# A value product moved into three norm stretches, relational maxima taken one by one, and a bank of their own for the first places

## The reference, cut to what matters

```python
# block 0, node layers (3 of them) and kernel attention; both start from the same xn
for l in range(L):
    msgs = nodes[src] + nodes[dst] + edge_proj
    agg = jax.ops.segment_sum(msgs, dst, num_segments=n)
    h = jnp.concatenate([nodes, agg], axis=-1) @ W1[l].T + b1[l]
    h = jax.nn.relu(_layernorm(h, ln_g[l], ln_b[l]))
    nodes = h @ W2[l].T + b2[l] + nodes
...
qkv = x @ qkv_w.T + qkv_b                       # x = xn: does not depend on the node layers
phi_q = jnp.exp(jnp.einsum('bhnd,md->bhnm', q, rf) - q_norm)
phi_k = jnp.exp(jnp.einsum('bhnd,md->bhnm', k, rf) - k_norm)
kv = jnp.einsum('bhnm,bhnd->bhmd', phi_k, v)
# block 1, relational attention, twice (4 heads, 1 head), 3 relations
alpha = jax.nn.leaky_relu(qi + kj, NEG_SLOPE)
m = jax.ops.segment_max(alpha, dst, num_segments=n_nodes)
e = jnp.exp(alpha - m[dst])
# block 3, experts: 16 experts each take their 64 best nodes
topk_score, topk_ids = jax.lax.top_k(scores.T, capacity)
xg = x[topk_ids]
```

## Time and profile before

| | |
|---|---|
| median of 3 runs | 4625.5 us |
| the profiled execution's own time | 4628.15 us |
| its span, first to last instruction | 4626.4 us |
| TensorE matmul busy | 4411.0 us (95%) |
| VectorE, ScalarE busy | 1027.6 us (22%), 1007.6 us (22%) |
| mean granted TensorE clock | 0.982 |
| data moved | 795.72 MB, mean 172 GB/s |

### The profile page before, as it was taken

One profiled execution on the slowest core, in us unless ns is written; L12 is line 12 of the kernel. 1 busy time (PEld: TensorE's weight loads), 2 busy tenths in 40 slices (PEclk: granted clock), 3 DMA queues, 4 the chain that ended last, 5 costly groups with the idle time before them and its releaser, 6 DMA issues.

```text
span 4626.4 us, 37973 instructions
## 1 busy us (share of the span) xinstructions
PE 4411.0 (95%) x15158; PEld 1976.2 (43%) x15183; DVE 1027.6 (22%) x1909; ACT 1007.6 (22%) x1830; POOL 89.9 (2%) x169
## 2 busy tenths in 40 slices
PE   8999999999999997989999999999999999999998
PEld 3444444444445543444444444443444334333333
DVE  6872011212311226123300000022542000000000
ACT  3121112323213326222210101012721000110000
POOL 1000000000000000000000000000000000000000
PEclk9999999999999998999999999999999999999999
DMA  9512222121271120113203031246128999999998
GB/s 323 158 69 87 77 64 81 60 68 60 110 314 64 46 82 1 46 37 105 69 27 100 23 100 36 91 188 254 39 82 342 409 423 423 414 423 407 413 413 355
DMA packets 128788, 795.72 MB, mean 172 GB/s; under 512 B 13951, under 2 KB 26543, under 8 KB 82173
## 3 DMA queue, kind: packets, MB, share of 16 engines
q1 hardware_dynamic: 116892, 728.07, 41.6%
q0 software_dynamic: 9280, 45.81, 2.6%
q10 hardware_dynamic: 2464, 19.67, 1.1%
HBM read 774.47 MB, written 56.83 MB: 180 GB/s over the span
## 4 chain that ended last, share of the span: by engine, by line
PE 87%; DMA 5%; DVE 4%; ACT 3%; issue 1%; POOL 0%; SPq 0%; ACTq 0%; DVEq 0%; POOLq 0%
PE bank L531 78%; DMA mem<-in_experts 4%; PE bank L682 4%; PE bank L529 3%; PE bank L656 2%; DVE mem L2380 1%; DVE mem L2376 0%; ACT mem L1694 0%; ACT mem L1715 0%; ACT mem L1856 0%; DVE mem L2045 0%; ACT mem L1352 0%; ACT mem L1730 0%; DVE rstd L2020 0%; ACT mem L1516 0%
## 5 line engine op out<-in xcount | busy, mean ns | idle before, releaser
L531 PE MATMUL bank<-mem 128*128 128x512 f32 (+5 forms) x11160 | 3538.0, 557 | 59.9 <-DMA mem<-in_experts 28.0
L531 PEld LDWEIGHTS bank<-mem 128*128 128x128 f32 (+3 forms) x11160 | 1485.3, 167 | 2030.7 <-issue 1900.7
L529 PE MATMUL bank<-ident,mem 128*128 128x128 f32 (+2 forms) x1484 | 221.3, 299 | 86.5 <-issue 25.0
L529 PEld LDWEIGHTS bank<-ident,mem 128*128 128x128 f32 (+2 forms) x1484 | 185.9, 155 | 175.6 <-issue 100.9
L1352 ACT ACTIVATE mem<-bank,cols 128x512 f32<-128x512 f32 (+1 forms) x88 | 60.4, 686 | 713.9 <-PE bank L531 713.9
L1352 ACT ACTIVATE mem<-bank 128x512 f32<-128x512 f32 x171 | 101.5, 597 | 511.4 <-PE bank L531 506.6
L682 PE MATMUL bank<-mem 128*128 128x512 bf16 x799 | 175.9, 379 | 0.9 <-issue 0.2
L531 PE MATMUL bank<-mem,ones 128*128 128x512 f32 (+1 forms) x344 | 153.9, 615 | 20.4 <-ACT mem L1386 11.6
L2674 DVE TENSOR_TENSOR mem<-mem,EV 128x512 f32<-128x512 f32 x48 | 33.2, 692 | 553.5 <-ACT EV L1957 553.5
L2652 DVE TENSOR_TENSOR mem<-mem,bank 128x512 f32<-128x512 f32 x48 | 33.0, 688 | 460.0 <-PE bank L531 460.0
L682 PEld LDWEIGHTS bank<-mem 128*128 128x128 bf16 x816 | 79.3, 98 | 97.4 <-DVE mem L2155 1.3
(11 more groups left out here) (363 smaller groups left out, 2107.6 us busy)
## 6 DMA issues: line engine op xcount, KB each, us to landing
mem<-in_experts SPq DMA_DIRECT2D x282, 1536.0 KB, 12.0
mem<-in_weights SPq DMA_DIRECT2D x329, 512.0 KB, 3.5
mem<-moe_up SPq DMA_DIRECT2D x30, 1152.0 KB, 9.0
mem<-moe_down SPq DMA_DIRECT2D x30, 1152.0 KB, 10.5
moe_up<-in_weights SPq DMA_DIRECT2D x16, 1152.0 KB
moe_down<-in_weights SPq DMA_DIRECT2D x16, 1152.0 KB
mem<-in_weights POOLq DMA_DIRECT2D x36, 384.0 KB, 7.8
mem<-in_experts ACTq DMA_DIRECT2D x6, 1536.0 KB, 14.7
```

The costliest lines, as they stand in the source:

```text
L529: ins = nc.tensor.transpose(out, lhsT, ident[0:lhsT.shape[0], 0:lhsT.shape[0]])
L531: ins = nc.tensor.matmul(out, lhsT, rhs, start=start, stop=stop)
```

## The change

Four edits go together. (1) The three turns of the node layers are written out on all three engines; the 36 products of v1 are spread over the three norms, 12 in each, in place of the 5 fillers: one before the last chunk's sum, two before the squares' sums, nine behind them. ScalarE empties the two v1 banks of a norm after its ReLUs, into a buffer of its own. The weight stream is read in the new order (`place_of`). The first layer's transposes no longer wait for VectorE. (2) In the kernel attention query and key of head 0 come before the transposes v1_tok on TensorE, and their emptying and squares before those of v1_tok on ScalarE. (3) VectorE takes the maxima of head 0 of a relation right behind that relation's key split. (4) The first pair's place transposes go to bank 7 and the second half of its gather to bank 5, so that the gather waits neither for the copy of the places nor for the copy of its first half.

```diff
+            def place_of(n):
+                layer, at = divmod(n - 2 * KC, 3 * KC + 2)
+                if n >= 2 * KC and layer < 3:
+                    if at < 2 * KC:
+                        return n - 2 * layer
+                    return V1_AT + 2 * layer + at - 2 * KC if at < 2 * KC + 2 else n - 2 * layer - 2
+                return n - KC if 2 * KC <= n < V1_AT + KC else n
-                    sp.dma_start(ring[:, n % RING, :], io["weights"][n + skipped]).then_inc(w_in[n % RING], 16)
+                    sp.dma_start(ring[:, n % RING, :], io["weights"][place_of(n) + skipped]).then_inc(w_in[n % RING], 16)
...
-            def norm_sums(label, source, last_ready, added=True):
+            def v1_steps(start, stop):
+                for n in range(start, stop):
+                    m, k = divmod(n, KC)
+                    if k == 0:
+                        state["v1"] = open_bank(), take_tile()
+                    out, slot = state["v1"]
+                    ins = mm(out[:, :], ring[:, slot, k * P:(k + 1) * P], XN[:, k, :], k == 0, k == KC - 1, k == KC - 1)
+                    if k == KC - 1:
+                        state["pending"] = tile_free
+                        ins.then_inc(bank_full.sem, bank_full.tick(("v1", m)))
+
+            def norm_sums(label, source, last_ready, added=True, v1_at=None):
...
+                if v1_at is not None:
+                    v1_steps(v1_at, v1_at + 1)
                 last_ready(KC - 1)
...
+                if v1_at is not None:
+                    v1_steps(v1_at + 1, v1_at + 3)
                 square_sums(label)
-                for k in range(FILL if label in ("lnh", "lny") else 0):
+                if v1_at is not None:
+                    v1_steps(v1_at + 3, v1_at + 2 * KC)
+                for k in range(FILL if label == "lny" else 0):
...
             def performer96():
-                linear("v1", KC, WHOLE, x_n)
-                by_chunk_tokens("v1_tok", chunks(C_), after(bank_free, "v1"))
+                linear(("mq", 0), 1, WHOLE, x_n, width=D8)
+                linear(("mk", 0), 1, WHOLE, x_n, width=D8)
+                by_chunk_tokens("v1_tok", v1_chunks, after(bank_free, "v1"))
...
-                        linear(("mq", h), 1, WHOLE, x_n, width=D8)
-                        linear(("mk", h), 1, WHOLE, x_n, width=D8)
...
-            with loop(pe, "gnn0", 3, (bank_full, tile_free, agg_done)):
-                to_tokens("tok0", chunks(A_), lambda m: pe.wait_ge(dve_done.sem, dve_done.at(("nodes", m), 1)))
...
-                norm_sums("lnh", chunks(B_), after(bank_free, "h0"))
-                linear("w2", KC, WHOLE, of(chunks(B_)), after(act_done, "relu0"))
-            state["tile"] += 2 * 3 * KC
+            for n in range(3):
+                tok, agg, hidden, relu = (("%s_%d" % (name, n)) for name in ("tok0", "agg0", "h0", "relu0"))
+                to_tokens(tok, chunks(A_), after(dve_done, "nodes_%d" % (n - 1)) if n else None)
...
+                norm_sums("lnh_%d" % n, chunks(B_), after(bank_free, hidden), v1_at=2 * KC * n)
+                linear("w2_%d" % n, KC, WHOLE, of(chunks(B_)), after(act_done, relu))
...
-                        ins = mm(bank[6][:, t * P:(t + 1) * P], place[p % 2][:, t, :], None, last=t == NT - 1, transpose=True)
+                        ins = mm(bank[6 if p else 7][:, t * P:(t + 1) * P], place[p % 2][:, t, :], None, last=t == NT - 1, transpose=True)
...
                 def gather(p, m):
-                    own = place[p % 2]
-                    if m == 0:
+                    own, out = place[p % 2], bank[5 if p == 0 and m >= 3 else 6]
+                    if p and m == 0:
                         pe.wait_ge(act_done.sem, act_done.at(("x_place_t", p)))
                     elif m == 3:
-                        pe.wait_ge(act_done.sem, act_done.at(("x_gather", p, 0)))
-                        group(bank[6][:, 3 * P:3 * P + 2], [(own[:, t, :], score_of[:, t, 2 * p:2 * p + 2]) for t in range(NT)], False)
+                        if p:
+                            pe.wait_ge(act_done.sem, act_done.at(("x_gather", p, 0)))
+                        else:
+                            pe.wait_ge(dve_done.sem, dve_done.at(("shared_hidden", 0)))
+                        group(out[:, 3 * P:3 * P + 2], [(own[:, t, :], score_of[:, t, 2 * p:2 * p + 2]) for t in range(NT)], False)
...
             def performer96():
                 s = float(D8) ** -0.5
-                linear("v1", KC, of(chunks(C_)), bias=bias_of("L0_mix_bv"))
+                act.wait_ge(dve_done.sem, dve_done.at("scaled_bias"))
...
+                queries_and_keys(0)
                 act.wait_ge(dve_done.sem, dve_done.at(("wo_x", KC - 1)))
...
-            with loop(act, "gnn0", 3, (bank_free, act_done)) as layer:
...
+            for layer in range(3):
...
+                for m in (2 * layer, 2 * layer + 1):
+                    act.wait_ge(bank_full.sem, bank_free.now(1))
+                    nc.scalar.activation(v1_chunks[:, m, :], filled()[:, :], ACT.Identity, bias=col("L0_mix_bv", m)).then_inc(
+                            bank_free.sem, bank_free.tick(("v1", m)))
+                linear("w2_%d" % layer, KC, of(chunks(C_)), bias=lambda m: col("L0_gnn_b2", layer * KC + m))
...
-            def edge_max(tag, h, relations, buf, at):
+            def relation_max(tag, h, r, buf, at):
 
...
+            def edge_max(tag, h, relations, buf, at):
+
+                for r in range(relations):
+                    relation_max(tag, h, r, buf, at)
+                row_max(tag, h, relations, at)
...
                 for r in range(relations):
                     split_keys(tag, heads, r)
-                edge_max(tag, 0, relations, 0, 0)
+                    relation_max(tag, 0, r, 0, 0)
+                row_max(tag, 0, relations, 0)
                 edge_weights(tag, 0, relations, True, 0)
```

87 lines of the change are left out of this document (44 added, 43 removed).

## The result

| | before | changed |
|---|---|---|
| median, first comparison | 4625.0 us (4 runs) | 4581.2 us (4 runs, 4577.0 to 4588.5) |
| ratio, 95% interval | | 0.9906 [0.9894, 0.9918] |
| the profiled execution's own time, its span | 4628.15, 4626.4 us | 4588.5, 4586.8 us |
| ratio in two later comparisons | | 0.9896 [0.9881, 0.9911], 0.9895 [0.9878, 0.9911] |
| medians of these two | 4625.8, 4625.0 us | 4576.9, 4577.2 us |

The forecast was 4585.9 us, range 4578 to 4595.

A forecast was written before the change was run, and what follows sets the result against it. TensorE's queue of matmuls, 87% of the chain, was taken as the bound. Terms -24.1 - 0.9 - 0.4 - 12.9 - 1.3 = -39.6 us took 4628.15 to 4588.5; less 2.65 to the median: 4585.9 us, range 4578 to 4595.

The forecast's parts named there:

- Norms: Node layers: first sum to w2 takes 17.24 us instead of 14.92, +2.32 per norm; 36 products leaving kernel attention give -31.0.
- the loop's edge: Node layers: writing out the loop counted as nothing, bounds -2 and +1 us over three turns.
- Head of the kernel attention: First transpose of v1_tok to features, 17.54 us, becomes 17.1 us: wait for squares replaced by ScalarE's emptyings, -0.4 us.
- Maxima: rgat1 and rgat2: exponentials start 6.35 and 6.55 us earlier, limited by the third relation's scores; -12.9 us in all.
- First places: First pair's gather: waits of 0.69 and 0.58 us go, -1.3 us; bounds 0 and -2.9.
- rival (c): Clock stays up after the gaps at kernel-attention features and first gather: 1.75 + 1.65 us more, 4582.5 us; chance 0.08.
- (a): Half clock from the kernel attention's head on, slowing norms and eight instructions behind the features: +2.2 us, 4588.1; chance 0.15.
- The rule that I weighed: Kernel attention's head: transposes don't count as clock-gate activity like matmuls, making half clock likely and the time 4588 us.
- (b): Relational maxima bring the naive 19.1 us, giving 4579.7 us; chance 0.06.
- (d): Weights of v1 come late in the norms: six tiles at 3.5 us, 21 us, giving 4606.9; chance 0.04.
- (f): Norms: v1's products wait, for example for a bank, and 1.44 + 1.60 us idling returns, 9.1 us, 4595; chance 0.05.
- (e): Without fillers the clock falls inside the norms, w2 at half clock: 31 us a layer, 93 in all, 4679; chance 0.02.

The follow-up runs named there:

- The run with half of the edit: Changed kernel with only the first places' transposes back in the gathers' bank, the second gather keeping its own bank; 4579.2 us in a single run.
- Two edits worth about 4 us: Changed kernel with head 1's query ahead of head 0's norms and the last relation's maximum taken tile by tile; 4569.7 us (0.9883), again 4576.2 us (0.9898).

## Why the prediction was right

**Norms: right.** TensorE sets the stretch, as the rows show, and the other engines' chain has slack; +2.14 us a norm, not +2.32. The stretch of 17.24 us that I had forecast measured 17.2. The distance from one layer's first sum to the next grew from 133.46 to 135.43 us, by 1.97; the 0.17 us between 2.14 and 1.97 are the loop's edge, which I had counted as nothing. Banks, weights and added emptyings cost nothing, as costed: there is no bracket on a row of any of the three norms.

**Head of the kernel attention: right in size, incomplete in reason.** 16.90 us against a forecast of 17.1, by the emptyings queued on ScalarE. What I missed is that edit 1 takes away the cover of v1_tok: with the order kept from before, the head took 2.4 us more than before, 1.6 of them the uncovered wait. The pair is worth 0.6 us, edit 2 beside edit 1 3.1 in one trace.

**Maxima: right**, and with the reason given. -13.1 us against -12.9; rgat1's gap 5.59 us, forecast 5.7.

**First places: the term that was mis-sized.** The 1.65 us for a clock that stays up was left out of the sum and put into rival (c); at this place it came in full: -3.4 us, beyond even the bound of -2.9. The 0.5 us beyond the bound are the waits again: their brackets are shorter than what they cost start to start. From the places' transposes to the first gather it was 1.32 us and is 0.47, 0.85 us for the wait of 0.69. Rows of before showed 4.57 against 2.92 us for the same 24 instructions, and I took the waits away without taking the slow clock with them. The run with half of the edit shows that the clock belongs to the wait of 0.69 us. At the other place of rival (c), the features, the clock was down in all three traces of the changed kernel, as I had assumed. That was the likelier case and not a certain one: of the nine traces with this head two kept it up.

**The rivals.** (a) did not come: the norms kept full speed (1.05 us) behind 24 transposes, in all nine traces with this head. The rule that I weighed, that transposes don't count as activity, would have had them slow, so the measurement stands against its use at this place. They were slow once (1.90 us), in the order with 24 matmuls ahead of them; the kernel before had that order and the same gap, and was not slow. What decides it stays open. (b) is out by the maxima's gaps. (c) came at one of its two places. (d) and (f) are out by the norms' rows. (e) has its mechanism (clock 0.55 behind an unfilled 5.83 us) and a price of 7 to 9 us where nothing fills; v1 does fill.

**The sum** by the rows is -43.1 us against -39.6, of which the first places are 2.1. The medians of three comparisons differ by 43.8, 48.8 and 47.8 us. Up to 6 us go beyond the rows. Stages that the change does not touch vary by as much from one execution to the next with one and the same kernel, so they can hold them; that they do is not shown. Three profiles of the changed kernel, start to start:

| stage | before | changed, first | second | third |
|---|---|---|---|---|
| first layer's experts | 97.5 | 100.4 | 97.5 | 97.8 |
| from there to rgat1's transposes | 395.0 | 388.9 | 386.9 | 387.1 |
| rgat2's transposes to the third layer's experts | 1056.5 | 1056.9 | 1051.0 | 1051.1 |

The first row's 3 us, in the first and then in the second profile:

```profile
1306.32 0.88 PE L541 MATMUL bank<-mem,pair_rows 2*128 2x384 f32 x2 [1.42 <-DMA mem<-moe_up]
1307.12 5.75 PE L541 MATMUL bank<-mem 128*64 128x384 f32 x24
```

```profile
1303.39 0.88 PE L541 MATMUL bank<-mem,pair_rows 2*128 2x384 f32 x2 [0.55 <-DMA mem<-moe_up]
1304.20 4.09 PE L541 MATMUL bank<-mem 128*64 128x384 f32 x24
```

TensorE waited 1.42 us for a load in place of 0.55, and the 24 instructions behind it took 5.75 us in place of 4.09. One profile of each kernel can therefore not place differences of 3 to 6 us in such stages. Why the later two comparisons favour the changed kernel more than the first stays open.

## What to carry to other kernels

Work that depends on nothing near it belongs into the gaps of a chain through other engines, in place of fillers; count its products against the gaps start to start, and ask what the moved work had been hiding where it stood. When a short wait goes, price the slow clock behind it together with it, from the rows right behind the wait, and look at more than one trace: at one place here the same code behind the same waits ran slow in seven traces and at full speed in two. And where a kernel's own stages vary by some us between executions, read an edit's worth from its rows, not from the total. Two edits worth about 4 us by the rows of one trace came out 6 to 11 us below the changed kernel by the ratios of one comparison, and between 4 us below and 1 us above it in the next.

## What the runs showed that I had not expected

- A wait of 0.69 us, behind one of 0.89 us and twelve small transposes, was followed by 24 gather instructions at 4.57 us in place of 2.85 (mean granted clock 0.61 with the wait alone and 1.00 in the changed kernel, windows below in this order), in all three traces that have this wait; in the eleven without it they took 2.84 or 2.85 us.

```profile
3451.20:3455.50 4.30, 4.30 (x24) 4.30 (x25) 0.00 (x0) 0.00 (x0) 0.00 (x0) 0.61 0.00 0
...
3460.40:3463.00 2.60, 2.60 (x26) 2.60 (x25) 0.00 (x0) 0.60 (x1) 0.00 (x0) 1.00 0.00 0
```

- The half clock does not return at the same point in every execution. The 128 instructions up to the end of head 0's key took 55.1 us in the first profile of the changed kernel and 56.3 us in the other two. The Trainium skill, "TensorE: Matmul & The Clock Gate", Part 1, says that one kernel measured different numbers of slow matmuls at its start, depending on the phase of the clock gate. These traces show such a variation in the middle of a kernel; they can't show where it comes from. The features' clock is a second case: in the three traces of the changed kernel the four instructions took 3.62, 2.74 and 2.69 us, and where they were quicker the next eight were slower (1.89, 2.87 and 2.92 us): the low clock began later and lasted as long.
- The hardware loop's edge cost hardly anything here: 0.17 us a turn. Written out, the next layer's transposes wait 0.96 us for VectorE in place of 1.05, and the aggregation 0.90 us for ScalarE in place of 0.97.
